# Own work orders for the first three and last four pipeline steps of a two-layer attention kernel, with setup memsets split and moved and the weights loaded in two pieces

## What is computed

```python
x = x + tanh(g_xattn) * xattn(layernorm(x), ctx)         # q from x, k and v from ctx, softmax, Wo
x = x + tanh(g_ffn)   * ffn(layernorm(x))
def ffn(x):
    h = rms(x, n1);  q, k, v = h @ wq.T, h @ wk.T, h @ wv.T      # q and k: rms over each head's 8
    x = x + mask32(causal_softmax(q k^T / sqrt(8)) v @ wo.T)
    xf = rms(x, n2);  p = softmax(xf @ gate.T);  w = top2(p) / sum(top2(p))
    o0 = gelu(xf @ e0_up.T) @ e0_down.T
    o1 = silu(xf @ e1_w1.T) * (xf @ e1_w2.T) @ e1_down.T
    o2 = gelu(gelu(gelu(xf @ l1.T) @ l2.T) @ l3.T) @ l4.T
    o3 = gelu(gelu(xf @ e3_down.T) @ e3_up.T) @ e3_out.T
    return x + mask32(w0*o0 + w1*o1 + w2*o2 + w3*o3)
```

## Time and profile before

| | us |
|---|---|
| median of 3 runs (lowest, highest) | 1200.54 (1198.05, 1200.64) |
| the profiled execution's own time | 1201.37 |
| its span | 1199.6 |
| PE busy | 1030.4 (86%) |
| DVE busy | 828.7 (69%) |
| ACT busy | 740.2 (62%) |
| POOL busy | 346.7 (29%) |
| mean granted TensorE clock | 0.954 of full speed |

### The profile page before, as it was taken

The page is one execution under the profiler, slowest core; times in us unless marked ns, Lnnn a source line. Parts: engine busy times, 40 slices in busy tenths (PEclk is TensorE's granted clock), DMA queues, the critical chain, the costliest instruction groups (busy, mean ns, idle before and its releaser), DMA issues. The chain is left out here.

```text
span 1199.6 us, 26646 instructions
## 1 busy us (share of the span) xinstructions
PE 1030.4 (86%) x8578; PEld 623.6 (52%) x8578; DVE 828.7 (69%) x2264; ACT 740.2 (62%) x1329; POOL 346.7 (29%) x513
## 2 busy tenths in 40 slices
PE   2365779999999899999989899999989899988797
PEld 1133445555556555555556555555556555555454
DVE  6237577777787877777787877777787777764523
ACT  1144466766676676766676776766676776755343
POOL 4610323314141513314141513214131514213030
PEclk9576789999999999999999999999999999999799
DMA  4325343343444434243444434243444433221300
GB/s 155 54 70 136 101 118 102 96 111 71 114 118 115 118 96 107 83 112 67 114 118 115 118 102 106 85 106 67 114 117 115 118 106 102 86 43 53 63 10 10
DMA packets 78549, 114.28 MB, mean 95 GB/s; under 512 B 9136, under 2 KB 41520, under 8 KB 78384
## 3 DMA queue, kind: packets, MB, share of 16 engines
q1 hardware_dynamic: 78368, 111.58, 36.7%
q10 hardware_dynamic: 144, 2.21, 0.5%
HBM read 58.97 MB, written 53.74 MB: 94 GB/s over the span
## 5 line engine op out<-in xcount | busy, mean ns | idle before, releaser
L701 ACT ACTIVATE probs<-ps_s2a 120x512 f32<-120x512 f32 (+1 forms) x256 | 152.9, 597 | 81.1 <-PE ps_s2a L1056 72.7
L822 DVE TENSOR_REDUCE mpadA<-ps_w 128x4 f32<-128x480 f32 x256 | 150.4, 651 | 54.7 <-PE ps_w L1038 54.7
L822 DVE TENSOR_REDUCE mpadB<-ps_w 128x4 f32<-128x512 f32 x256 | 158.8, 683 | 29.1 <-PE ps_w L1038 29.1
L701 ACT ACTIVATE probs<-ps_s2b 120x512 f32<-120x512 f32 (+1 forms) x256 | 152.5, 596 | 0.0
L1103 PE MATMUL ps_w<-W,hid 128*128 128x96 f32 x1024 | 129.9, 281 | 15.1 <-ACT hid L697 10.9
L608 POOL TENSOR_SCALAR_AFFINE_SELECT probs<-probs 128x1024 f32<-128x1024 f32 x128 | 140.1, 1094 | 0.0
L1103 PEld LDWEIGHTS ps_w<-W,hid 128*128 128x128 f32 x1024 | 120.6, 194 | 36.2 <-issue 26.2
L574 POOL TENSOR_TENSOR rB<-veB,neg_half 128x4 f32<-128x4 f32 x16 | 16.1, 1008 | 400.9 <-DVE veB L725 400.9
L1121 PE MATMUL ps_w<-xfT,W 128*128 128x512 f32 x160 | 85.1, 621 | 0.0
L697 ACT ACTIVATE hid<-ps_s2a 128x512 f32<-128x512 f32 x80 | 47.8, 598 | 51.6 <-PE ps_s2a L1114 39.7
L1056 PE MATMUL ps_s2a<-qdA,kstA 128*120 128x512 f32 x128 | 69.4, 542 | 11.4 <-DMA qdA<-mTA 5.0
(11 more groups left out here) (184 smaller groups left out, 2119.6 us busy)
## 6 DMA issues: line engine op xcount, KB each, us to landing
scratch_Aq<-split_q SPq DMA_DIRECT2D x48, 256.0 KB, 2.4
qdA<-scratch_Aq SPq DMA_DIRECT2D x64, 192.0 KB
scratch_Bq<-split_q SPq DMA_DIRECT2D x48, 256.0 KB, 2.4
scratch_Bk<-split_k SPq DMA_DIRECT2D x48, 256.0 KB, 3.0
qdB<-scratch_Bq SPq DMA_DIRECT2D x64, 192.0 KB
kstB<-scratch_Bk SPq DMA_DIRECT2D x64, 192.0 KB
scratch_Ak<-split_k SPq DMA_DIRECT2D x48, 240.0 KB, 2.9
kstA<-scratch_Ak SPq DMA_DIRECT2D x64, 180.0 KB
```

What stands on the lines that cost most here:

```text
L701: nc.scalar.activation(probs[0:k, slot_of(part, *index), :], bank[0:k, :], ACT.Exp, scale=SCALE if part == "A" else 1.0).then_inc(done, 1)
L822: nc.vector.tensor_reduce(mneg[OP[part]][:, :, c, b], bank[:, 0:HT * k].rearrange("p (h k) -> p h k", h=HT), AX.X, ALU.max, negate=True).t ...
```

## The change

The works stay the same ones, and each engine's instructions for a work too. What changes:

- `Step` takes an order of its own, and banks are dealt out by that order. Steps 0, 1, 15, 16, 17 and 18 get new orders. Step -1 and step 2 keep the order of `SCHEDULE` with the absent parts left out, with banks dealt anew. The loop is untouched.
- `qd["A"]` is cleared half on VectorE, half on GpSimd in the first `N norm`. The clearing of `qd["B"]` and `kst["B"]` moves behind the power of the second `N norm`, and the wait for `kd` goes.
- SyncE issues the load of x before it waits for `kd`, not after.
- The weights are loaded by two DMAs: the four matrices of cross-attention, then the rest, for which the first `B qk` waits.

The diff, without the lines that only replace `BANK[...]` by `st.bank[...]`:

```diff
+def first_group():
+    return [use for use in SCHEDULE if use[0] == "N"]
+def second_group():
+    return (one("N", "load", 0, None)
+            + estimate("A", 0) + estimate("A", 1) + estimate("A", 2) + estimate("A", 3) + one("A", "mT")
+            + one("N", "stats", 0, None) + exact("A", 0, 0) + exact("A", 0, 2)
+            + exact("A", 1, 0) + one("N", "norm", 0, None) + exact("A", 1, 2) + values("A", 0)
+            + exact("A", 2, 0) + one("N", "xT") + exact("A", 2, 2) + values("A", 1)
+            + exact("A", 3, 0) + one("A", "oT", 0, "t") + exact("A", 3, 2) + values("A", 2)
+            + one("A", "nT", 0, "t") + one("A", "wo", 0, "t") + values("A", 3)
+            + one("A", "oT", 1, "t") + one("A", "nT", 1, "t") + one("A", "wo", 1, "t")
+            + one("A", "stats", 0, None) + one("N", "base", 0, None)
+            + one("N", "q") + one("N", "v") + one("N", "k") + one("A", "norm", 0, None) + one("A", "hT"))
+def third_group():
+    return (one("N", "load", 0, None)
+            + estimate("A", 0) + one("B", "qk", 0) + one("B", "qk", 1) + one("B", "qk", 2) + one("B", "qk", 3)
+            + estimate("A", 1) + one("B", "squares", 0, None) + one("B", "sums", 0, None)
+            + estimate("A", 2) + one("B", "root", 0, None) + one("B", "scale", 0, None) + estimate("A", 3)
+            + one("A", "mT") + one("B", "qT") + one("B", "kT") + one("N", "stats", 0, None)
+            + exact("A", 0, 0) + one("B", "v") + exact("A", 0, 2) + one("N", "norm", 0, None)
+            + exact("A", 1, 0) + estimate("B", 0) + exact("A", 1, 2)
+            + one("B", "init", 0, None) + one("B", "copy", 0, None) + values("A", 0)
+            + exact("A", 2, 0) + one("N", "xT") + exact("A", 2, 2) + values("A", 1)
+            + exact("A", 3, 0) + one("A", "oT", 0, "t") + estimate("B", 1) + exact("A", 3, 2) + values("A", 2)
+            + one("A", "nT", 0, "t") + one("A", "wo", 0, "t") + values("A", 3)
+            + one("A", "oT", 1, "t") + one("A", "nT", 1, "t") + one("A", "wo", 1, "t")
+            + one("A", "stats", 0, None) + one("N", "base", 0, None) + estimate("B", 2)
+            + one("N", "q") + one("N", "v") + one("N", "k") + one("A", "norm", 0, None) + estimate("B", 3)
+            + one("A", "hT") + one("B", "mT"))
+def of_parts(parts, order=None):
+    return [use for use in order or SCHEDULE if use[0] in parts]
+def last_cross_attention():
+    return (of_parts("ABDM", self_attention() + second_experts() + cross_attention())
+            + fill("D", "e1_w1", 0, "w") + one("A", "wo", 0, "t") + fill("D", "e1_w2", 0, "w") + values("A", 3) + estimate("B", 3)
+            + one("D", "gates", 0, None) + fill("D", "e1_w1", 1, "w") + one("A", "oT", 1, "t") + fill("D", "e1_w2", 1, "w")
+            + one("A", "nT", 1, "t") + fill("D", "e2_l1", 0) + one("A", "wo", 1, "t") + one("A", "stats", 0, None)
+            + fill("D", "e2_l1", 1) + one("D", "gates", 1, None) + one("B", "mT") + fill("D", "e3_down", 0)
+            + one("A", "norm", 0, None) + fill("D", "e0_up", 0) + one("A", "hT") + one("D", "gates", 2, None)
+            + fill("D", "e0_up", 1, "w") + one("D", "gates", 3, None) + one("D", "gates", 4, None))
+def last_self_keys():
+    return (exact("D", 0, 0) + down(1) + exact("D", 0, 2)
+            + one("B", "qk", 0) + one("B", "qk", 1) + one("B", "qk", 2) + one("B", "qk", 3)
+            + exact("D", 1, 0) + one("B", "squares", 0, None) + values("D", 0) + exact("D", 1, 2)
+            + one("B", "sums", 0, None) + down(0) + exact("D", 2, 0) + values("D", 1) + exact("D", 2, 2)
+            + one("D", "oT", 0, "t") + exact("D", 3, 0) + one("D", "nT", 0, "t") + values("D", 2) + exact("D", 3, 2)
+            + one("B", "root", 0, None) + one("D", "wo", 0, "t")
+            + fill("M", "e2_l2", 0) + one("B", "scale", 0, None) + fill("M", "e2_l2", 1) + values("D", 3)
+            + fill("M", "e3_up", 0) + one("B", "qT") + one("B", "kT") + one("D", "oT", 1, "t") + fill("M", "e3_up", 1)
+            + one("D", "nT", 1, "t") + fill("M", "e2_l3", 0) + estimate("B", 0) + one("D", "wo", 1, "t")
+            + one("D", "out", 0, None) + one("D", "squares", 0, None) + fill("M", "e2_l3", 1, "w")
+            + estimate("B", 1) + down(2) + one("D", "norm", 0, None) + one("B", "init", 0, None) + one("B", "copy", 0, None)
+            + one("B", "v") + estimate("B", 2) + down(3) + one("M", "store", 0, None) + one("D", "xfT")
+            + estimate("B", 3) + one("D", "logits") + fill("D", "e1_w1", 0, "w") + fill("D", "e1_w2", 0, "w") + one("B", "mT")
+            + one("D", "gates", 0, None) + fill("D", "e1_w1", 1, "w") + fill("D", "e1_w2", 1, "w")
+            + fill("D", "e2_l1", 0) + one("D", "gates", 1, None) + fill("D", "e2_l1", 1) + fill("D", "e3_down", 0)
+            + one("D", "gates", 2, None) + fill("D", "e0_up", 0) + fill("D", "e0_up", 1, "w")
+            + one("D", "gates", 3, None) + one("D", "gates", 4, None))
+def last_self_values():
+    return (exact("D", 0, 0) + down(1) + exact("D", 0, 2) + exact("D", 1, 0) + down(0) + exact("D", 1, 2) + values("D", 0)
+            + exact("D", 2, 0) + values("D", 1) + exact("D", 2, 2) + one("D", "oT", 0, "t")
+            + exact("D", 3, 0) + one("D", "nT", 0, "t") + values("D", 2) + exact("D", 3, 2) + one("D", "wo", 0, "t")
+            + fill("M", "e2_l2", 0) + fill("M", "e2_l2", 1) + values("D", 3) + fill("M", "e3_up", 0) + one("D", "oT", 1, "t")
+            + fill("M", "e3_up", 1) + one("D", "nT", 1, "t") + fill("M", "e2_l3", 0) + one("D", "wo", 1, "t")
+            + one("D", "out", 0, None) + one("D", "squares", 0, None) + fill("M", "e2_l3", 1, "w")
+            + down(2) + one("D", "norm", 0, None) + one("D", "xfT") + down(3) + one("M", "store", 0, None) + one("D", "logits")
+            + fill("D", "e1_w1", 0, "w") + fill("D", "e1_w2", 0, "w") + one("D", "gates", 0, None)
+            + fill("D", "e1_w1", 1, "w") + fill("D", "e1_w2", 1, "w") + fill("D", "e2_l1", 0) + one("D", "gates", 1, None)
+            + fill("D", "e2_l1", 1) + fill("D", "e3_down", 0) + one("D", "gates", 2, None)
+            + fill("D", "e0_up", 0) + fill("D", "e0_up", 1, "w") + one("D", "gates", 3, None) + one("D", "gates", 4, None))
+def last_experts():
+    return (down(1) + fill("M", "e2_l2", 0) + fill("M", "e2_l2", 1) + down(0) + fill("M", "e2_l3", 0) + fill("M", "e2_l3", 1, "w")
+            + fill("M", "e3_up", 0) + fill("M", "e3_up", 1) + down(2) + down(3) + one("M", "store", 0, None))
...
-RAMP = [(-1, "N"), (0, "NA"), (1, "NAB"), (2, "NABD")]
+RAMP = [(-1, "N", first_group()), (0, "NA", second_group()), (1, "NAB", third_group()), (2, "NABD", of_parts("NABD"))]
 LOOP = (3, NG - 1)
-TAIL = [(NG - 1, "ABDM"), (NG, "BDM"), (NG + 1, "DM"), (NG + 2, "M")]
+TAIL = [(NG - 1, "ABDM", last_cross_attention()), (NG, "BDM", last_self_keys()),
+        (NG + 1, "DM", last_self_values()), (NG + 2, "M", last_experts())]
+assert all(sorted(map(str, order)) == sorted(map(str, of_parts(parts))) for _, parts, order in RAMP + TAIL)
...
-    for t, parts in RAMP:
-        step(Step(t, parts))
+    for t, parts, order in RAMP:
+        step(Step(t, parts, order))
     with engine.Fori(*LOOP) as t:
-        step(Step(t, PARTS))
+        step(Step(t, PARTS, SCHEDULE))
...
+        ATTENTION = sum(n for _, n in WCOLS[:4])
...
                             sp.wait_ge(x1_base, g)
+                        sp.dma_start(xt[:], x[bass.ds(g * G, G), :, :].rearrange("b t d -> t b d")).then_inc(x_loaded, 16)
+                        if not st.first("N"):
 
                             sp.wait_ge(kd_ready["A"], g)
-                        sp.dma_start(xt[:], x[bass.ds(g * G, G), :, :].rearrange("b t d -> t b d")).then_inc(x_loaded, 16)
                         sp.dma_start(ctT[:], ctxT[:, bass.ds(g * CT, CT)]).then_inc(ctx_loaded, 16)
...
-                            sp.wait_ge(a_cleared, 1)
+                            sp.wait_ge(a_cleared, 2)
...
                         pool.tensor_tensor(rsA[:], veA[:], neg_half[:], ALU.pow).then_inc(a_rstd, 1)
                         if st.first("N"):
 
-                            pool.wait_ge(kd_ready["A"], 1)
+                            pool.memset(qd["A"][:, HT // 2:HT].bitcast(F32), 0.0).then_inc(a_cleared, 1)
+                        elif st.parts == "NA":
+
                             pool.memset(qd["B"][:].bitcast(F32), 0.0)
                             pool.memset(kst["B"][:].bitcast(F32), 1.0).then_inc(b_cleared, 1)
...
-            act.dma_start(W[:], weights).then_inc(weights_loaded, 16)
+            act.dma_start(W[:, 0:ATTENTION], weights[:, 0:ATTENTION]).then_inc(weights_loaded, 16)
+            act.dma_start(W[:, ATTENTION:], weights[:, ATTENTION:]).then_inc(rest_loaded, 16)
...
-            nc.vector.memset(qd["A"][:].bitcast(F32), 0.0)
+            nc.vector.memset(qd["A"][:, 0:HT // 2].bitcast(F32), 0.0)
...
                     elif (part, work) == ("B", "qk"):
+                        if st.first("B") and index == 0:
```

(21 more changed lines are left out.)

79 lines of the change are left out of this document (39 added, 40 removed).

## The result

The changed kernel takes **1212.3 us** (median of 4 runs, 1210.9 to 1213.1) where the kernel before took 1199.7 beside it: a ratio of 1.010, with a 95% interval of 1.0086 to 1.0115. I had forecast 1199.8 with a range of 1190 to 1206. The change is slower by 12.5 us and the time lies outside the range. Its profiled execution spans 1211.0 us, 11.4 more than the span before.

What follows compares the result with a forecast made beforehand. TensorE was taken to bound full steps, the chain of dependences those outside the loop. Terms 2.3 + 2.2 - 5.8 + 1.3 - 0.8 = -0.8 us against the profiled 1201.37 gave a median of 1199.8, range 1190 to 1206.

Steps and rivals of the forecast that it cites:

- Start and step 0: Start to second norm: shift of -9.0 us, TensorE's 9.27 us wait at the transpose gone; first exact scores at 43.9.
- Step 1, first half: First half of step 1: exact scores start at 95.2, a shift of -11.4 us; second statistics 12.4 us earlier.
- W: End of the last `wo` in step 1: 128.1 us before, forecast at 115.75.
- Step 1, second half: End of step 1: gain given back, mTB landing 8 us behind stack loads; step 2 starts at 140.0, 2.3 us later.
- rival (1): End of step 1: mTB passes the stack loads, lands 1.9 us after issue; 4.5 us less, 1195.3; chance 0.13.
- Step 15: Estimate 3 of B ahead of the last `oT` puts 2.48 us of reduces before the last division: +2.2 us.
- Step 16: Tail step of 63.4 us before: fills and Gelus run until 57.6 us, mTB hidden; -5.8 us.
- Rival (4): Steps 15 and 16: TensorE's clock halves, 5 us more, 1204.8; decided before the second estimate block; chance 0.25.
- Steps 17 and 18: Last two tail steps: +1.3 us from a transpose's wait and later exponentials, then -0.8 us from a filled gap.
- my two tests: Wrong if step 2 starts before 135 us, or the four tail steps save more than 8 us or nothing.
- (2): At the start: GpSimd's memset does not hold VectorE; 3 us less, 1196.8; chance 0.15.
- (3): Tail packs tighter than the walk, halfway to TensorE's own work; 5.5 us less, 1194.3; chance 0.15.

Runs made afterwards that it cites:

- the later gaps filled: Changed kernel with unused matmuls (9, 3, 3, 3 and 3) in TensorE's later gaps of step 16, the 3.39 us gap left open: 1204.9 us.
- the kernel with the division first: Changed kernel with the last transposes of D's output and divided values ahead of the q and k transposes in step 16: 1202.2 us.

## Why the prediction was wrong

**Start and step 0: right.** The scaling ended at 14.98 as the row of the copy beside it had suggested, the exact scores came at 43.99 (43.9), the transpose at 52.41 (52) without its 9.27 us. That +1.5 met +1.6 is partly luck, though: `kd` beside GpSimd took 2.69 us, 1.6 more and not 0.35, while the scaling ended 0.7 us later than before and not 1.15, and from the last maxima to the first exact scores it took 0.7 us less. The experiments add what I had not separated: the setup alone gives nothing, and the memset placed where it was costs some 3 us that a later place gives back.

**Step 1, first half: right.** Exact scores at 95.45 (95.2). The last `wo`, with VectorE's sum behind it, was through at 116.65 where I had 115.75 (W).

**Step 1, second half: right in kind, short in size.** That mTB stands behind the stack loads, in the queue and in landing, is shown by SyncE's order alone, worth 7.5 us. Step 2 starts 6.1 us later than before and not 2.3, and the 3.8 us between have four parts. W itself was 0.9 us late. The loads' issue began at W+13.4 instead of W+12.4, since the low part of k was through 0.7 us later and its stores (issued at 126.30) took 3.7 instead of 3.4 us. The issue of the eight loads lasted 3.8 instead of 3.4 us, so mTB went out at W+17.2, not W+15.8. The last 1.5 us are an error of the sum. The landing was what I took from the rows of x: 7.9 us in the median and 8.3 at the most, against 8. But mTB is four stores of 8 KB each, issued one after the other in 2.41 us, and I counted the 8 us from the first of them. Alone, with a landing of 1.9 us, it was 3.8 us from first issue to exact scores; with 8 us in place of the 1.9 this gives 9.9, which is what was measured, where I had 8.4. For the same reason rival (1) was priced at 4.5 us less and should have had 6. It is excluded: mTB did not pass the loads. And the larger point stood in my own numbers without a price: the new order of step 1 gives the whole gain of the steps before it back. In the traces a lead of 11.1 us at its exact scores is a lag of 6.1 at its end; as a run it costs 15 us (1192.0 to 1206.9).

**Step 15: right**, +1.7 where +2.2 stood.

**Step 16: wrong, and this decides the sign.** The step of the prediction that failed is the term of -5.8 us: 57.6 us, walked forward with durations at the full clock, and with a last division that waits on VectorE but costs TensorE nothing. It took 68.0. From the first to the fourth block of maxima I had 15.0 us (32 to 47.0). On VectorE it was 21.0 in the changed kernel,

```profile
1112.08 2.49 DVE L921 TENSOR_REDUCE mpadB<-ps_w 128x4 f32<-128x512 f32 x4 [4.29 <-PE ps_w L1139]
...
1133.06 2.49 DVE L921 TENSOR_REDUCE mpadB<-ps_w 128x4 f32<-128x512 f32 x4 [1.67 <-PE ps_w L1139]
```

and 15.6 in the same order with the later gaps filled:

```profile
1111.49 2.48 DVE L921 TENSOR_REDUCE mpadB<-ps_w 128x4 f32<-128x512 f32 x4 [4.12 <-PE ps_w L1147]
...
1127.06 2.49 DVE L921 TENSOR_REDUCE mpadB<-ps_w 128x4 f32<-128x512 f32 x4 [0.92 <-PE ps_w L1147]
```

So what the walk lacked between the blocks is the clock: filled, the whole step takes 59.6 us, and 8.4 of the 10.3 us are gone. In the 2.0 that are left (59.6 after 57.6) TensorE still waits 3.40 us for the division and runs slow for 3 us behind it. I had written that the division stands behind the low parts and `kd`, and had not followed this on to TensorE. That the kernel with the division first takes 57.2, within 0.4 of my walk, does not bear the walk out, since that is another order.

Rival (4) named this clock and its price at 5 us with a chance of 0.25. Its decision point was right in place (the projection at 39.5 us into the step is the first slow one of the long stretch). Its price was low by some 3 us: the projections, the logits and the transpose cost what I had (1.7 each, 0.8 and 0.5), but the first fills behind the logits cost 2.9 and not 0.3 (3.76 and 3.02 us, in the division-first kernel 1.96 and 1.88), and v (1.97 instead of 1.08) and the blocks of estimates were not in it. My "against", that TensorE has more work between the gaps, did not hold: at full clock the work stands in pieces of 0.6 to 3 us between gaps of 0.85.

**Steps 17 and 18: right in sign**, +0.5 and -0.5 for +1.3 and -0.8.

Of my two tests, step 2 did not start before 135 (143.7), and the four tail steps saved nothing: they cost 6.2 us. The second said that I am wrong. Rivals (2) and (3) are excluded too: (2) by the scaling, which took 4.08 us beside the memset and 1.11 with the clearing moved later, (3) by the length of step 16. The range failed since its upper end held rival (4) or a late mTB, not both: 1199.8 + 3.8 + 10.3 - 1.8 for the loop and the steps 15, 17 and 18 gives 1212.1, and 1212.3 were measured.

## What to carry to other kernels

A new order of works has to be priced on every in-order list that walks it: here the same list that freed TensorE put four small stores behind 1488 KB of loads on SyncE, and one local swap on that engine gave 7.5 us back. When a DMA's landing goes into a sum, count it from the last issue of the batch and not from the first. Where a chain leaves TensorE a row of sub-microsecond gaps, cost the stretch at both clock levels. Idle matmuls in such gaps are a quick test of that cost before a new order: they gave 3.2 to 7.4 us in the changed kernel and 3.2 in the kernel before, where the next step took part of it back. When a change bundles several moves, run them one by one: this bundle of -8, +15 and +5 us looked like +12.

## What was not expected of the hardware

- In step 16 the granted clock stayed at 0.50 (1125 to 1135) while TensorE paused for 0.84 to 0.87 us at a time, with no pause over 2.14 us in the ten us before; behind the one wait of 3.40 us it was slow for some 3 us only.
- The same kernel fell into two groups of times, 1201 to 1203 us eight times and 1206.5 to 1212.6 four times, where its gaps were of that size.
- A memset of GpSimd's holds VectorE's scaling for its whole length (4.08 and 9.24 instead of 1.11 us), through two memsets in a row (6.92 and 1.80 us), but not a memset of VectorE's (1.66 us inside it).
- Four stores of 8 KB each took 7.9 us (median) from issue to landing right behind 1488 KB of loads, and 1.9 us when issued ahead of them; from the first issue to the first use it was 9.9 and 3.8 us.
